# Decays ahead of heads, seven shared banks and warming matmuls in a Mamba, attention and expert layer

## The chip, the cores and the metric

The kernel runs on one core of a Trainium2 chip. The metric is the device time of one execution in microseconds. The core has TensorE (PE; its weight loads are shown as PEld), VectorE (DVE), ScalarE (ACT), GpSimd (POOL) and SyncE (SP, which here only issues transfers). Each engine takes its instructions in the order of its own list and waits on semaphores. TensorE writes to eight PSUM banks of 128 x 512 f32.

## The reference

One decoder layer on x of shape (8, 256, 512), in f32:

```python
x = x + ssm(layernorm(x))                       # Mamba-2: 64 heads of 16, state 128, chunks of 128
x = x + cross_attention(layernorm(x), ctx, ctx) # 32 query heads of 16 on 8 key heads, softmax
x = x + top2_experts(layernorm(x))              # 8 experts, gelu(gate) * up, then down
```

In the first part each chunk of 128 tokens needs, for each head, a 128 x 128 matrix of decays exp(cum_i - cum_j) times C·B, and this matrix times x. In the second, the scores are shifted by each row's maximum before the exponential. In the third, each token goes to two of eight experts.

## The kernel before

The work is cut into pieces such as `("decay", s)` or `("score", i)`. A list `ORDER` holds all pieces of the first two parts. Every engine walks the same list and executes its share of each piece, so the list sets the order on every engine, and a piece that waits holds up all that is behind it on its engine. `mixer_slots` (L95) and `attention_slots` (L234) give each piece a slot number. `whole_order` (L322) sorts them.

**The first part, the mixer** (up to about 600 us) has 32 units: batch b, chunk c and half hf of the heads. A unit has eight steps s, each for four heads, 256 in all. The pieces of a step are: `decay` (L639, a bf16 matmul of 60 rows into a bank of its own, four a round), `bound` (ACT L739, which reads the bank and so frees it), `exp` (ACT L743), `mix_v` or `mix_g` (DVE or POOL, both L748, the product with C·B), and `heads` (L651, for two steps at once, 16 matmuls of 32 columns, which add into a bank that the whole unit shares and that is freed by `yz`, DVE L902). Every fourth slot is a round: the heads of steps i-7 and i-5, then the four decays i to i+3. Around the rounds stand the projections (`x`, `z`: L565), the output projection (`out`: L631), transposes (L570), `x_turn` read by `xdt` (DVE L882), and `ones` (L623), which needs `square` (ACT L733) and `fold` (POOL L950, L951).

**The start of the attention** overlaps the mixer's end. For batch 0 the keys are loaded by `ctx_in` (SP L1483), behind the eight loads of `ecum_in` (SP L1006). `k_hi` (ACT L1122, L1123) waits for this load, `k_lo` (POOL L1430) for k_hi, and `k_turn` (PE L570) for k_lo. The piece `freed` makes ACT and DVE wait for the last projection `z` of the last batch.

**The attention** does 32 items a batch. Side by side run the scores of batch b (`score` L1069, `exponent` ACT L1150, `product` L1078 once in four items) and the row maxima of batch b+1 (`max` L1055, `max_fold` DVE L1250). In the middle of a batch the maxima of half the heads are ready: `nmax` (DVE L1257) and `n_turn` (PE L1061). Beside them the finished batch b-1 goes to the router: `r_stats` (DVE L1287), `r_newton` (14 small POOL instructions), `r_xn` (ACT L1169), `r_turn` (PE L570), `r_logit` (L1095). At the end of the last batch three `keep_warm` pieces do matmuls of ones whose result nobody reads (L1024).

**Banks.** `shared_banks` (L217) walks `ORDER` and gives each piece that writes PSUM the bank that was freed longest ago, with a wait for the piece that reads it last. So any change of order also changes which reader each piece waits for. Mixer and attention pieces share all eight.

**The experts** (from about 940 us) come behind the list, with 39 tiles of tokens.

Of the kernel before, what the change touches and what calls it, by code (L numbers as in the profile page):

```python
# [41 lines left out]
GROUP = 4  # L42
NDECAY = 10
BANKS = 8
# [50 lines left out]
def mixer_slots():  # L95
# [3 lines left out]
    def put(s, *pieces):  # L99
        slots.setdefault(s, []).extend(pieces)  # L100

    for i in range(NS_STEPS + 2 * GROUP):
        if i % GROUP == 0:
            for s in range(i - 2 * GROUP + 1, i - GROUP, 2):
                if s >= 0:
                    put(i, ("heads", s))
            for s in range(i, min(i + GROUP, NS_STEPS)):
                put(i, ("decay", s))
        if 0 <= i - 3 < NS_STEPS:
            put(i, ("mix_v" if (i - 3) % 2 else "mix_g", i - 3))  # L110
        if 0 <= i - 2 < NS_STEPS:
            put(i, ("exp", i - 2))
        for s in range(NS_STEPS):
            if i == s - s % GROUP + s % GROUP // 2:
                put(i, ("bound", s))
# [73 lines left out]
DMA_ONLY = {"ecum_out", "ecum_in", "freed", "mixed", "cum_out", "cum_in", "ctx_in", "n_out", "router_in", "first_expert", "r_store", "out_in", "c_weight_out"}  # L189


def bank_use(stage, *key):
# [12 lines left out]
    if stage == "keep_warm":  # L205
        return (stage, *key), (stage, *key)
# [10 lines left out]
def shared_banks(order, size, use):  # L217

    at = {piece: n for n, piece in enumerate(order)}
    bank, opened_after, last = {}, {}, [None] * size  # L220
    for n, piece in enumerate(order):
        used = use(*piece)
        if used and used[0] not in bank:
            k = min(range(size), key=lambda i: -1 if last[i] is None else at[last[i]])
            if last[k] is not None:
                assert at[last[k]] < n, (piece, last[k])
                opened_after[piece] = last[k]
            bank[used[0]], last[k] = k, used[1]
    return bank, opened_after


def attention_slots():
# [20 lines left out]
    for b in range(NB):  # L253
# [19 lines left out]
        for h in range(2):  # L273
            put(n * (b - 1) + n // 2 * (h + 1) - LEAD + 1, ("nmax", b, h))
            at = n * (b - 1) + n // 2 * (h + 1) - LEAD + 3
            put(at, ("n_turn", b, h))
# [46 lines left out]
def whole_order():  # L323
# [3 lines left out]
    def among(a):  # L327
        for at, end, first, width in ((-54, -40, NS_STEPS - 20, 9), (-40, -33, NS_STEPS - 11, 4.9), (-33, -1, NS_STEPS - 3, 19)):
            if at <= a < end:
# [5 lines left out]
              -25: [("k_hi", 0, 0), ("k_lo", 0, 0)], -24: [("k_hi", 0, 1), ("k_lo", 0, 1)]}  # L335
# [11 lines left out]
def layer_kernel(nc, A, out):  # L347
# [12 lines left out]
    with ExitStack() as top:  # L360
# [81 lines left out]
        work_bank, work_after = shared_banks(ORDER, BANKS, bank_use)  # L442
# [584 lines left out]
        def tensor_attention(e, piece):  # L1027
            stage, *key = piece
            if stage == "keep_warm":
                e.wait_ge(*done("exponent", NB * N_ITEMS - 1))  # L1030
                repeated(e, work(*piece), key[1]).then_inc(piece_done[stage], 1)
# [753 lines left out]
```

## Time and profile before

| | us |
|---|---|
| median of 3 runs | 1380.18 |
| lowest and highest | 1377.15, 1388.65 |
| the profiled execution | 1391.4 |
| its span | 1389.6 |
| its mean granted TensorE clock | 0.948 |

In the rows below, a row of a timeline has its start and duration in us, the engine, the line, what is written and read, and how many instructions it joins. In square brackets stands how long the engine was idle before it and what ended that. A row of windows gives for a stretch its length, then the busy us of each engine with the count of its instructions, then the granted TensorE clock as a share of 2.4 GHz (0.50 is 1.2 GHz), the share of DMA time and GB/s.

### The profile page before, as it was taken

The page shows a single profiled execution, that of the slowest core. Times are in us where ns is not written, and L with a number is a line of the kernel's source. Part 1 is how long each engine was busy: PE and PEld are TensorE (multiplying, and loading weights), DVE is VectorE, ACT ScalarE, POOL GpSimd, SP SyncE. Part 2 cuts the span into 40 slices and gives each one's busy share as a digit, 9 for nine tenths or more (in the row PEclk, how much of TensorE's full clock was granted, in tenths as well). Part 3 has the DMA queues.
Part 4 walks back from the last instruction along what each step waited for, and adds up shares of the span by engine and source line. Part 5 has one row for each costly group of instructions (what it writes and reads, how often), then busy time and mean ns, then how long its engine had stood idle before and what let it go on. Part 6 is the DMA issues. An engine that isn't in the chain of part 4 may idle for free.

```text
span 1389.6 us, 22701 instructions
## 1 busy us (share of the span) xinstructions
PE 1296.1 (93%) x7601; PEld 735.4 (53%) x7601; DVE 823.6 (59%) x1847; ACT 696.2 (50%) x1334; POOL 595.3 (43%) x913
## 2 busy tenths in 40 slices
PE   6799999999999989788999988889999999999996
PEld 4567676766766666443444433234444444444443
DVE  6898989888888877588888789561111111111111
ACT  2768686867676765645777776621111111111110
POOL 1475657566666657672333334641222222222221
PEclk9999999999999999889899898669999999999998
DMA  9100000000000001002111100113344244334222
GB/s 346 31 11 18 11 20 11 19 11 19 9 21 10 21 9 28 1 5 102 36 35 36 36 32 32 33 54 109 67 137 138 56 137 141 89 94 137 47 46 30
DMA packets 49553, 77.31 MB, mean 56 GB/s; under 512 B 19168, under 2 KB 32224, under 8 KB 48416
## 3 DMA queue, kind: packets, MB, share of 16 engines
q1 hardware_dynamic: 39504, 52.43, 10.9%
q0 software_dynamic: 8736, 20.61, 7.7%
q10 hardware_dynamic: 1200, 2.82, 0.5%
q8 instruction: 64, 1.05, 0.3%
q14 instruction: 49, 0.40, 0.1%
HBM read 152.97 MB, written 20.25 MB: 125 GB/s over the span
## 4 chain that ended last, share of the span: by engine, by line
PE 64%; DVE 22%; issue 5%; POOL 4%; ACT 3%; DMA 1%; SPq 1%; POOLq 0%; DVEq 0%; ACTq 0%
PE work_ps L565 10%; PE gate_ps L1563 10%; PE up_ps L1563 10%; PE down_ps L1547 9%; PE work_ps L631 7%; DVE maxes L1250 5%; PE work_ps L570 4%; PE work_ps L1078 3%; DVE conv L752 3%; PE mturn_ps L570 2%; DVE decay L748 2%; PE work_ps L1069 2%; PE work_ps L651 2%; PE work_ps L1055 1%; PE work_ps L1095 1%
## 5 line engine op out<-in xcount | busy, mean ns | idle before, releaser
L565 PE MATMUL work_ps<-xnT,w_in 128*128 128x256 f32 (+1 forms) x1216 | 288.1, 385 | 6.1 <-DVE xdt L882 2.8
L565 PEld LDWEIGHTS work_ps<-xnT,w_in 128*128 128x128 f32 (+1 forms) x1216 | 226.3, 192 | 59.5 <-issue 21.5
L748 POOL TENSOR_TENSOR decay<-decay,cbm 128x512 f32<-128x512 f32 x128 | 184.2, 1442 | 128.5 <-ACT decay L743 127.2
L1651 POOL DMA_INDIRECT out_dram<-y_out,ids x39 | 61.9, 1588 | 335.0 <-DVE row_w L1615 231.7
L1250 DVE TENSOR_REDUCE maxes<-work_ps 128x2 f32<-128x512 f32 x256 | 164.5, 681 | 33.5 <-PE work_ps L1055 32.6
L1630 DVE TENSOR_TENSOR act<-gelu,up_ps 128x512 f32<-128x512 f32 x39 | 26.8, 687 | 253.0 <-PE up_ps L1563 253.0
L1150 ACT ACTIVATE prob<-work_ps 128x512 f32<-128x512 f32 x256 | 142.7, 613 | 52.0 <-PE work_ps L1069 52.0
L743 ACT ACTIVATE decay<-decay 128x512 f32<-128x512 f32 x256 | 161.5, 638 | 12.8 <-DVE xnT L1201 5.3
L739 ACT ACTIVATE decay<-work_ps 128x512 f32<-128x512 f32 x256 | 138.8, 601 | 40.6 <-PE work_ps L639 40.1
L1563 PE MATMUL gate_ps<-w_e,xgT 128*128 x312 | 141.0, 595 | 0.9 <-issue 0.9
L1547 PE MATMUL down_ps<-w_e,actT 128*128 x312 | 140.4, 593 | 0.8 <-ACT actT L1593 0.8
L1563 PE MATMUL up_ps<-w_e,xgT 128*128 x312 | 140.3, 592 | 0.0
L748 DVE TENSOR_TENSOR decay<-decay,cbm 128x512 f32<-128x512 f32 x128 | 121.1, 949 | 29.6 <-ACT decay L743 29.6
L631 PE MATMUL work_ps<-w_out,yz 128*128 128x512 f32 x256 | 128.5, 625 | 2.2 <-DVE yz L902 1.4
L1055 PE MATMUL work_ps<-kT,qT 48*128 48x256 f16 x512 | 94.8, 297 | 8.3 <-ACT qT L1144 2.9
L1622 DVE TENSOR_SCALAR y_out<-down_ps,row_w 128x512 f32<-128x512 f32 x39 | 29.3, 750 | 122.3 <-PE down_ps L1547 122.3
L1563 PEld LDWEIGHTS up_ps<-w_e,xgT 128*128 128x128 f32 x312 | 59.3, 190 | 74.6 <-issue 74.6
L752 DVE SCALAR_TENSOR_TENSOR conv<-work_ps,conv_w,conv 128x255 f32<-128x255 f32 (+2 forms) x240 | 97.4, 468 | 0.7 <-ACT conv L705 0.5
L1069 PE MATMUL work_ps<-qT,kT 49*128 49x512 f16 x256 | 92.2, 430 | 1.7 <-ACT prob L1150 0.6
L1078 PE MATMUL work_ps<-prob,v_aug 128*32 128x512 f32 x512 | 81.8, 716 | 11.0 <-DVE kT L1240 7.8
L1580 ACT ACTIVATE xgT<-mturn_ps 128x512 f32<-128x512 f32 x39 | 23.3, 597 | 137.0 <-PE mturn_ps L570 137.0
L1593 ACT ACTIVATE actT<-mturn_ps 128x512 f32<-128x512 f32 x39 | 23.3, 597 | 128.4 <-PE mturn_ps L570 128.4
(267 smaller groups left out, 1922.6 us busy)
## 6 DMA issues: line engine op xcount, KB each, us to landing
w_e<-c_experts_dram SPq DMA_DIRECT2D x39, 3072.0 KB
normed_tokens<-r_xn SPq DMA_DIRECT2D x17, 256.0 KB, 2.4
out_dram<-x_sb SPq DMA_DIRECT2D x17, 256.0 KB, 2.8
eexp<-ecum_scratch SPq DMA_DIRECT2D x64, 64.0 KB
x_sb<-x_dram SPq DMA_DIRECT2D x1, 3072.0 KB, 15.8
w_in<-c_w_inT_dram ACTq DMA_DIRECT2D x1, 2560.0 KB, 12.5
w_in<-c_w_inT_dram SPq DMA_DIRECT2D x1, 2048.0 KB, 8.1
w_out<-c_w_outT_dram SPq DMA_DIRECT2D x1, 2048.0 KB, 21.5
```

What stands on the lines that cost most here:

```text
L565: m = e.matmul(ps[0:width, at:at + L], w_in[:, k, col:col + width], xnT[b % 2][:, k, :], start=(k == 0), stop=(k == KD - 1))
L631: m = e.matmul(work(stage, tile)[:, :], yz[tile % 2][:, ct, :], w_out[:, ct, :], start=(ct == 0), stop=(ct == NCZ - 1))
L739: e.activation(decay[s % NDECAY][:, :], work("decay", s)[:, :], ACT.Relu, scale=-1.0).then_inc(piece_done[stage], 1)
L743: e.activation(decay[s % NDECAY][:, :], decay[s % NDECAY][:, :], ACT.Exp, scale=-1.0).then_inc(piece_done[stage], 1)
L748: return e.tensor_tensor(four(decay[s % NDECAY]), four(decay[s % NDECAY]), cb, ALU.mult)
L752: return e.scalar_tensor_tensor(o, work("x", b, j)[:, i * L:(i + 1) * L - late], conv_w[:, 2 * j + i, TAPS - 1 - late:TAPS - late], o, ALU ...
L1069: e.matmul(work(*piece)[:, :], kT[b % 3][base:base + PARTS + 1, k, t * P:(t + 1) * P], qT[b % 3][base:base + PARTS + 1, 2 * k:2 * k + 2, : ...
L1078: m = e.matmul(work("pv", b, s % N_ITEMS // 8)[32 * q:32 * q + 32, :], v_aug[b % 2][:, t, 4 * kh + q, :], prob[(s - 3 + q) % 12][:, :], st ...
L1150: e.activation(prob[s % 12][:, :], work("score", s)[:, :], ACT.Exp, scale=DH ** -0.5).then_inc(piece_done[stage], 1)
L1250: e.reduce_max(maxes[b % 2][:, t, first:first + 2], work("max", b, p)[:, :].rearrange("p (h t) -> p h t", h=2), AX.X).then_inc(piece_done[ ...
L1547: m = e.matmul(down_ps[i % 2][:, :], actT[i % 2][:, k, :], w_e[:, bass.ds(place[i], 1), k, 2 * EH:].rearrange("p o n -> p (o n)"), start=( ...
L1563: m = e.matmul(ps[:, :], xgT[i % 2][:, k, :], w_e[:, bass.ds(place[i], 1), k, off:off + EH].rearrange("p o n -> p (o n)"), start=(k == 0), ...
```

## The change

It has three edits.

1. In each round the four decays come before the two pairs of heads.
2. In `whole_order`, `k_hi` and `k_lo` of batch 0 move from slots -25 and -24 to -21 and -20, one round later.
3. `shared_banks` gets a list of banks for each piece: mixer pieces may take all eight, attention pieces the first seven. The eighth is written by matmuls that nobody reads: the three `keep_warm` pieces, which no longer wait for a bank, and six new `warm` pieces of five matmuls, one for each batch from 2 to 7, right before its first `n_turn`.

```diff
@@ mixer_slots
         if i % GROUP == 0:
+            for s in range(i, min(i + GROUP, NS_STEPS)):
+                put(i, ("decay", s))
             for s in range(i - 2 * GROUP + 1, i - GROUP, 2):
                 if s >= 0:
                     put(i, ("heads", s))
-            for s in range(i, min(i + GROUP, NS_STEPS)):
-                put(i, ("decay", s))
@@ shared_banks
-            k = min(range(size), key=lambda i: -1 if last[i] is None else at[last[i]])
+            k = min(allowed(*piece), key=lambda i: -1 if last[i] is None else at[last[i]])
@@ attention_slots
+            if b > 1 and h == 0:
+                put(at, ("warm", b, 5))
             put(at, ("n_turn", b, h))
@@ whole_order
-              -25: [("k_hi", 0, 0), ("k_lo", 0, 0)], -24: [("k_hi", 0, 1), ("k_lo", 0, 1)]}
+              -21: [("k_hi", 0, 0), ("k_lo", 0, 0)], -20: [("k_hi", 0, 1), ("k_lo", 0, 1)]}
@@ layer_kernel
-        work_bank, work_after = shared_banks(ORDER, BANKS, bank_use)
+        work_bank, work_after = shared_banks(ORDER, BANKS, bank_use, lambda stage, *key: range(BANKS if stage in MIXER else BANKS - 1))
@@ tensor_attention
             if stage == "keep_warm":
                 e.wait_ge(*done("exponent", NB * N_ITEMS - 1))
-                repeated(e, work(*piece), key[1]).then_inc(piece_done[stage], 1)
+                repeated(e, work_ps[BANKS - 1], key[1])
+            elif stage == "warm":
+                e.wait_ge(*done("r_init"))
+                repeated(e, work_ps[BANKS - 1], key[1])
```

The changed kernel is three lines longer from L1029 on, so its L1058 is L1055 of before.

TensorE in the round of decays 132 to 135, in the mixer's fifth batch (L651 is heads, L639 the decays, L565 a projection; the brackets name what each waits for). Before:

```order
L623 MATMUL work_ps<-ones,squares 128x1 [waits fold,bound]
L651 MATMUL work_ps<-decay,xdt 32x128 [waits mix_v,mix_g]
L651 MATMUL work_ps<-decay,xdt 32x128 x7
L651 MATMUL work_ps<-decay,xdt 32x128 [waits mix_v,mix_g]
L651 MATMUL work_ps<-decay,xdt 32x128 x7
L639 MATMUL work_ps<-RT,LT 128x512 [waits bound]
L639 MATMUL work_ps<-RT,LT 128x512 [waits taps]
L639 MATMUL work_ps<-RT,LT 128x512 [waits xn_copy]
L639 MATMUL work_ps<-RT,LT 128x512 [waits xdt]
L565 MATMUL work_ps<-xnT,w_in 128x256 [waits carried]
```

After:

```order
L623 MATMUL work_ps<-ones,squares 128x1 [waits fold,bound]
L639 MATMUL work_ps<-RT,LT 128x512 [waits bound]
L639 MATMUL work_ps<-RT,LT 128x512 [waits taps]
L639 MATMUL work_ps<-RT,LT 128x512 [waits xn_copy]
L639 MATMUL work_ps<-RT,LT 128x512 [waits xdt]
L651 MATMUL work_ps<-decay,xdt 32x128 [waits mix_v,mix_g]
L651 MATMUL work_ps<-decay,xdt 32x128 x7
L651 MATMUL work_ps<-decay,xdt 32x128 [waits mix_v,mix_g]
L651 MATMUL work_ps<-decay,xdt 32x128 x7
L565 MATMUL work_ps<-xnT,w_in 128x256 [waits carried]
```

The decays moved ahead of the heads. The last of them opens its bank behind `xdt`, and now the heads stand behind that wait.

ScalarE at the start of the attention (L1122 and L1123 are `k_hi`, L743 and L739 exp and bound of the mixer, L733 the square, L720 a tanh of z). Before:

```order
L720 ACTIVATE zs<-work_ps 128x512
L1122 ACTIVATE xbc<-xbc 128x16x16
L1123 ACTIVATE xbc<-xbc 128x16x16
L743 ACTIVATE decay<-decay 128x512
L739 ACTIVATE decay<-work_ps 128x512 x2
L733 ACTIVATE squares<-yz 128x512
L1122 ACTIVATE xbc<-xbc 128x16x16
L1123 ACTIVATE xbc<-xbc 128x16x16
L743 ACTIVATE decay<-decay 128x512
L739 ACTIVATE decay<-work_ps 128x512 x2
```

After, from the second instruction behind the same L720 on (L1125 is `k_hi` now):

```order
L739 ACTIVATE decay<-work_ps 128x512 x2
L733 ACTIVATE squares<-yz 128x512
L743 ACTIVATE decay<-decay 128x512
L739 ACTIVATE decay<-work_ps 128x512 x2
L743 ACTIVATE decay<-decay 128x512
L726 ACTIVATE state<-work_ps 128x512
L1135 ACTIVATE xn<-x_sb,a_rows 128x512
L1141 ACTIVATE xbc<-xn 128x32x16
L743 ACTIVATE decay<-decay 128x512
L720 ACTIVATE zs<-work_ps 128x512
L1125 ACTIVATE xbc<-xbc 128x16x16
L1126 ACTIVATE xbc<-xbc 128x16x16
```

Two bounds, exponentials, the square and the state's copy now come before the first `k_hi`, which stands behind the second L720.

TensorE at the first `n_turn` of batch 2 (L1061, after L1064), with the product (L1078, L1081), a score (L1069, L1072) and a max (L1055, L1058). Before:

```order
L1055 MATMUL work_ps<-kT,qT 128x256 [waits max_fold]
L1055 MATMUL work_ps<-kT,qT 128x256
L1078 MATMUL work_ps<-prob,v_aug 32x512 [waits exponent,k_copy]
L1078 MATMUL work_ps<-prob,v_aug 32x512 x3
L1061 MATMUL work_ps<-ident,nmax 16x128 [waits nmax,exponent]
L1061 MATMUL work_ps<-ident,nmax 16x128
L1069 MATMUL work_ps<-qT,kT 128x512 [waits max_fold]
L1055 MATMUL work_ps<-kT,qT 128x256 [waits exponent]
L1055 MATMUL work_ps<-kT,qT 128x256
```

After:

```order
L1058 MATMUL work_ps<-kT,qT 128x256 [waits k_copy]
L1058 MATMUL work_ps<-kT,qT 128x256
L1081 MATMUL work_ps<-prob,v_aug 32x512 [waits exponent]
L1081 MATMUL work_ps<-prob,v_aug 32x512 x3
L1024 MATMUL work_ps<-m_ones 128x512 [waits r_init]
L1024 MATMUL work_ps<-m_ones 128x512 x4
L1064 MATMUL work_ps<-ident,nmax 16x128 [waits nmax,max_fold]
L1064 MATMUL work_ps<-ident,nmax 16x128
L1072 MATMUL work_ps<-qT,kT 128x512 [waits exponent]
L1058 MATMUL work_ps<-kT,qT 128x256 [waits max_fold]
L1058 MATMUL work_ps<-kT,qT 128x256
```

The five matmuls of ones (L1024) come between product and `n_turn`. The wait for `k_copy` moved from the product to the max ahead of it.

## Rows read from the trace of the kernel before

**Rows 1.** The page: the span, and the clock granted in 40 slices.
```profile
span 1389.6 us, 22701 instructions
...
PEclk9999999999999999889899898669999999999998
```

**Rows 2.** Windows by stage: mixer, attention, end of the attention.
```profile
50.00:500.00 450.00, 439.30 (x3390) 310.35 (x3389) 384.38 (x725) 329.64 (x651) 284.44 (x399) 1.00 0.06 15
...
640.00:870.00 230.00, 208.45 (x1633) 96.92 (x1629) 195.95 (x497) 169.72 (x323) 75.50 (x180) 0.87 0.14 47
...
884.00:915.00 31.00, 29.65 (x114) 10.57 (x111) 10.54 (x50) 16.70 (x32) 15.63 (x39) 0.50 0.10 35
```

**Rows 3.** Timeline of all engines, 543 to 563 us, where the attention starts.
```profile
547.00 0.59 ACT L720 ACTIVATE zs<-work_ps 128x512 f32<-128x512 f32 x1
...
548.63 1.95 PE L631 MATMUL work_ps<-w_out,yz 128*128 128x512 f32 x4 [0.90 <-DVE yz L902]
...
549.76 3.57 SPq L1483 DMA_DIRECT2D xbc<-ctx_dram  x2
...
552.94 0.42 ACT L1122 ACTIVATE xbc<-xbc 128x256 f16<-128x256 f32 x1 [5.35 <-DMA xbc<-ctx_dram]
...
560.07 0.56 PE L623 MATMUL work_ps<-ones,squares 128*128 128x1 f32 x2 [2.97 <-POOL squares L951]
```

**Rows 4.** Windows with TensorE alone (length, busy us, clock, DMA, GB/s).
```profile
559.87:566.70 6.83, 6.63 (x42) 0.50 0.00 0
```

**Rows 5.** Waits of TensorE from 50 to 500 us: total, times, longest.
```profile
PE work_ps L651 <- DVE decay L748: 4.8, 7, 1.2
```

**Rows 6.** Timeline of TensorE in the round of decays 120 to 123.
```profile
297.61 0.65 PE L651 MATMUL work_ps<-decay,xdt 128*32 128x128 f32 x16 [0.65 <-DVE decay L748]
298.18 0.60 PE L639 MATMUL work_ps<-RT,LT 60*128 60x512 bf16 x4
```

**Rows 7.** Timeline of all engines in the round of decays 132 to 135.
```profile
324.91 0.74 DVE L882 TENSOR_TENSOR xdt<-work_ps,dt_tok 128x256 f32<-128x256 f32 x2
...
326.30 1.99 PE L565 MATMUL work_ps<-xnT,w_in 128*128 128x256 f32 x8 [0.21 <-DVE eexp L889]
```

**Rows 8.** Windows of the attention by half batches, all engines.
```profile
679.00:697.00 18.00, 17.68 (x123) 9.46 (x123) 11.58 (x26) 10.93 (x19) 2.66 (x7) 0.72 0.20 67
697.00:714.00 17.00, 14.87 (x131) 6.22 (x129) 16.76 (x45) 15.29 (x33) 7.69 (x17) 1.00 0.01 1
714.00:731.00 17.00, 15.81 (x121) 8.48 (x120) 11.30 (x26) 10.63 (x19) 2.74 (x8) 0.80 0.21 71
...
782.00:799.00 17.00, 16.97 (x112) 8.80 (x109) 10.17 (x26) 8.83 (x15) 3.25 (x10) 0.61 0.21 72
...
851.00:870.00 19.00, 16.12 (x84) 7.13 (x84) 17.34 (x60) 8.27 (x16) 12.93 (x34) 0.65 0.16 57
```

**Rows 9.** Timeline of TensorE around the first `n_turn` of batch 3.
```profile
712.33 1.06 PE L1078 MATMUL work_ps<-prob,v_aug 128*32 128x512 f32 x8 [1.63 <-DVE kT L1240]
...
716.48 0.72 PE L570 MATMUL work_ps<-ident,r_xn 128*128 128x128 f32 x4 [0.87 <-ACT r_xn L1169]
```

**Rows 10.** Windows with TensorE alone: stretches at half clock behind that place.
```profile
681.40:686.16 4.76, 4.76 (x24) 0.50 0.55 201
716.88:720.30 3.42, 3.42 (x18) 0.50 0.48 177
...
856.25:860.24 3.99, 3.98 (x18) 0.50 0.38 133
```

**Rows 11.** Timeline of all engines, attention, first half of a batch.
```profile
738.67 2.10 ACT L1150 ACTIVATE prob<-work_ps 128x512 f32<-128x512 f32 x4
...
738.74 1.06 PE L1078 MATMUL work_ps<-prob,v_aug 128*32 128x512 f32 x8
...
739.61 2.48 DVE L1250 TENSOR_REDUCE maxes<-work_ps 128x2 f32<-128x512 f32 x4
```

**Rows 12.** Timeline of TensorE: the matmuls of ones at full clock.
```profile
933.17 3.18 PE L1024 MATMUL work_ps<-m_ones 128*128 128x512 bf16 x14
```

More of the change, by code:

```diff
@@ L188, in mixer_slots @@
     return slots
-DMA_ONLY = {"ecum_out", "ecum_in", "freed", "mixed", "cum_out", "cum_in", "ctx_in", "n_out", "router_in", "first_expert", "r_store", "out_in", "c_weight_out"}
+DMA_ONLY = {"ecum_out", "ecum_in", "freed", "mixed", "cum_out", "cum_in", "ctx_in", "n_out", "router_in", "first_expert", "r_store", "out_in", "c_weight_out", "keep_warm", "warm"}
 def bank_use(stage, *key):
@@ L204, in bank_use @@
         return ("score", *key), ("exponent", *key)
-    if stage == "keep_warm":
-        return (stage, *key), (stage, *key)
     if stage == "q_turn":
@@ L214, in bank_use, with shared_banks @@
     return ((stage, *key), (read_by[stage], *key)) if stage in read_by else None
-def shared_banks(order, size, use):
+def shared_banks(order, size, use, allowed):
     at = {piece: n for n, piece in enumerate(order)}
```

## The prediction

> **What bounds the kernel now.** The page comes first: its line of the clock shows full speed in the mixer and in the experts, and less only in slices 19 to 28, about 560 to 950 us [rows 1]. The windows by stage tell who sets the pace. From 50 to 500 us TensorE is busy 439.3 of 450 us at clock 1.00: it is the bound, and only the other 10.7 us can be won there without taking work from it [rows 2]. In the attention nobody is busy all the time: TensorE 208 and VectorE 196 of 230 us, at clock 0.87. The half batches split this up. From 697 to 714 us VectorE works 16.76 of 17 us at full clock, so the maxima set the pace. In 679 to 697 and 714 to 731 us TensorE is busy almost throughout, at 0.72 and 0.80, and VectorE only 11.6 and 11.3 us: there TensorE sets it, and part of its time is the clock's [rows 8]. This pattern comes back each batch. The experts' stage is TensorE at full clock throughout, and the change leaves it alone. Last, the timeline where the attention starts shows one long stall: ScalarE sits 5.35 us for the load of the context [rows 3].
>
> **The k_hi move.** The load is issued at 549.76, behind the loads of `ecum_in`, and lands at 552.9; ScalarE has been free since 547.59. Behind the waiting `k_hi` stand the exponential, two bounds and the square, behind the square the fold on GpSimd, and behind the fold TensorE's `ones`, which waits 2.97 us until 560.07 [rows 3]. Then the clock is at half for 6.83 us, in which TensorE is busy 6.63 [rows 4]; what it did before the fall was to be idle. In the new order two exponentials, four bounds, the square and the state's copy come before `k_hi`. The square then runs at about 549.2, since `yz` is done at 548.6, and the fold is over by 551, before TensorE reaches `ones` at 557.1. `k_hi` comes behind a tanh that needs a projection ending at 557.1, 4 us after the landing, so its wait is gone, not moved. Next in line is `k_turn`, which needs `k_lo`; TensorE reaches it only some ten microseconds behind `ones`. Up to there everything shifts by 2.97 us, plus half of 6.83 us if the clock stays up: **-6.4 us**. If the clock falls anyway it is -3.0. If what follows is late for another reason, 0.
>
> **The decays ahead of the heads.** No instruction is added. Four decays take 0.60 us [rows 6], two pairs of heads about 1.0. It gains where TensorE stands before heads for `mix_v`, for the decays now fill that time, at most 0.60 us of it. The waits of 50 to 500 us have 4.8 us of this kind in 7 places [rows 5], one of them in [rows 6]. The shortest is filled whole with 0.3, one with 0.5 and five with 0.6: 3.8 us. It loses where a decay's bank opens late, as the heads are then behind it. In the round of decays 132 to 135 the last decay needs `xdt`, which ends at 325.65. The heads then end at about 326.7, while the next projection has started at 326.30 [rows 7]: 0.4 lost. This stands alike in batches 4, 5 and 6, and two rounds with `xdt` or `yz` late lose 0.3 and 0.6: 2.1 us in all. Waits behind 500 us are followed by another wait that ends at the same time, so they bring nothing. Net **-1.7 us**. Ends: -5, if earlier decays also bring ScalarE's chain forward so that all 4.8 us go, and +2, if nothing is filled.
>
> **Seven banks.** I took each piece of the attention with the piece that now frees its bank and looked in the trace when that one ended. Most end long before. In the halves set by VectorE some do not. At 738.74 TensorE starts a product [rows 11]. It now waits for the exponential that starts at 738.67 and ends at 739.3, 0.6 later. Product and score then push the next max to an end of 740.96, where VectorE started its fold at 740.21 (it is in the four from 739.61): 0.8 us late. The other late ones of that half, 0.2 to 0.6, hide in this one, for everybody behind has already shifted. Batches 2 to 5 give 0.8 each, batch 6 1.3, batches 1 and 7 0.35 each: **+5.2 us**. Ends: 0, if ScalarE is ahead by as much, and 2.6 a batch, some 16, if they add up. In the halves set by TensorE no opening is late. The Trainium skill (TensorE: Matmul & The Clock Gate, A second HAM failure mode: psum-queue depth-cycling) says that a kernel that cycles through PSUM banks lets TensorE pause between groups so often that its clock swings. This trace does not agree for the halves set by VectorE: with TensorE busy 14.87 of 17 us in many pauses they keep 1.00 [rows 8]. By the row the banks cost 5.2 us, by the rule the price would be that of rival D.
>
> **The warming matmuls.** Fourteen take 3.18 us at full clock [rows 12], so five take 1.1 us, twice that at half clock, and there are six such blocks. Each stands before `n_turn`, and behind it waits the same batch's r_turn. That one could not start before `r_xn`: TensorE stood 0.87 us for it [rows 9], and 0.3 us just before. So 1.2 us of pauses hide 1.1 us of matmuls, where the pauses are as here. I take **+1 us** for all six. With no cover it is +6.6.
>
> **The clock behind them.** In the second halves the clock falls twice: once behind the pauses of 1.63 and 0.87 us [rows 9], once later, among transposes and the router's small matmuls. The block of ones falls into the first place only. From `r_turn` on, the time at half clock there is 4.76, 3.42 and 3.99 us [rows 10], and twice 3.41 in the batches between; one batch has no fall. TensorE is busy throughout, so half of these 19 us comes back: **-9.5 us**. Ends: 0, and all that the clock costs in the second halves: busy time by one minus clock is 5.0, 3.2, 3.2, 6.6 and 5.6 us [rows 8], the second 3.2 being the half from 748 us, which looks like the one from 714: 23.5 us.
>
> **Sum.** -6.4 - 1.7 + 5.2 + 1.0 - 9.5 = -11.4 us. The profiled execution took 1391.4 us, so 1380.0. It is 0.8% above the median of the three. A likely place is the end of the attention, 31 us at clock 0.50 with TensorE busy 29.65 [rows 2]: at full clock 14.8 us of TensorE and 16.7 of ScalarE could be some 14 us shorter, and the three runs differ by 11.5. Nothing in the change touches it directly. I keep the ratio: 1380.18 x 1380.0 / 1391.4 = 1369.
>
> **Rivals.** A is the forecast, at 1361 to 1378 us: 0.45.
>
> B: with the first fall gone TensorE enters the second place earlier and the clock holds there too. The whole 23.5 us come back: -6.4 - 1.7 + 5.2 + 1.0 - 23.5 = -25.4, 1355 us. Against it: the second fall came with TensorE fully busy, so no pause made it. 0.15.
>
> C: the ones do not hold the clock, since the stretch behind them is thin as well. -1.9 us, 1378. For it: one half batch stayed at half clock for two falls in a row, at 0.61 [rows 8]. 0.20.
>
> D, slower: seven banks keep VectorE waiting. With 16 us instead of 5.2 and no clock won it is -6.4 - 1.7 + 16 + 1 = +8.9, 1389 us. If the pauses also pull the clock of the halves at 1.00 to 0.80, 14.87 us of TensorE become 18.6, 1.6 more than the 17 us, six times: +18.5, 1398. It decides from 1.2 us lost a batch on (six times 1.2 against 8.1 - 1). The skill's section named above speaks for it. Against it are the long leads in the rows before. 0.12.
>
> E: the k_hi move brings nothing, for the chain behind it was late anyway: 1375 us. 0.08.
>
> **From this to the numbers.** A measurement of this kernel can tell about 1%, 14 us, from no change. Below 1366.4 us lies all of B, nearly half of A and a little of C: 0.39. Above 1394 lies part of D: 0.05. The rest is 0.56. The range from 1353 to 1389 leaves out the lower part of B and the upper half of D, and spans the bounds of the clock and of the banks.
>
> **What would show it.** ScalarE without a wait for the context, and `ones` without a pause, with the clock at 1.00 from 560 to 567 us. From 50 to 500 us some 2 us less, with few waits of heads. `max_fold` with waits of up to 0.8 us in the first halves. At each block of ones a product, five matmuls, then `n_turn`, and the next stretch at full clock; a half there would mean C. What would make the forecast wrong most is the clock: where it falls hangs on small shifts, here and at the attention's end.

## The result, with the profile after

The changed kernel takes 1391.89 us (median of 20 runs) against 1385.89 us for the kernel before (20 runs, the same hours). The ratio is 1.0044, with a 95% interval from 1.0025 to 1.0064: 6 us slower, where 11 faster were forecast. The profiled execution took 1390.9 us, and that of before 1391.4. The latter was a slow one of its kind (the runs of before span 1377 to 1394, and the slower ones have the lower mean clock), so the two traces differ by 0.5 us, and the other way. Below, the traces say where time goes, and the ratios say how much the whole is worth.

The page of the changed kernel, its span and its clock:

```profile
span 1389.1 us, 22758 instructions
...
PEclk9999999999999999978999998889999999999999
```

The same three windows as in [rows 2]:

```profile
50.00:500.00 450.00, 433.84 (x3325) 304.64 (x3324) 380.58 (x715) 323.50 (x639) 279.50 (x394) 1.00 0.06 15
640.00:870.00 230.00, 205.71 (x1651) 92.79 (x1652) 197.30 (x493) 170.94 (x324) 71.98 (x175) 0.93 0.14 47
884.00:915.00 31.00, 25.65 (x142) 9.21 (x141) 17.30 (x76) 18.55 (x37) 21.61 (x48) 0.84 0.10 35
```

TensorE, the mixer's bound, is busy 433.8 of 450 us there, where it was 439.3: it waits more, though the edit was to fill its waits. The attention's clock went from 0.87 to 0.93, as meant, but the stretch does not get through more work: the scores 0 to 208 take 215.5 us before and 215.9 after.

**The mixer.** From the first `out` (L631) to that of tile 13 the kernel before took 458.95 us (89.60 to 548.55), and the changed one 468.00 (90.40 to 558.40). The groups of TensorE in these stretches: instructions, busy us, mean ns, then the idle time before them and what ended it. Before:

```profile
L631 PE MATMUL work_ps<-w_out,yz 128*128 128x512 f32 x208 | 101.3, 609 | 1.3 <-DVE yz L902 0.5
L651 PE MATMUL work_ps<-decay,xdt 128*32 128x128 f32 x1664 | 57.8, 276 | 7.0 <-DVE decay L748 7.0
L639 PE MATMUL work_ps<-RT,LT 60*128 60x512 bf16 x208 | 33.0, 381 | 0.3 <-DVE yz L902 0.3
```

After:

```profile
L631 PE MATMUL work_ps<-w_out,yz 128*128 128x512 f32 x208 | 101.3, 609 | 4.6 <-DVE yz L902 4.6
L651 PE MATMUL work_ps<-decay,xdt 128*32 128x128 f32 x1664 | 57.7, 276 | 2.1 <-DVE yz L902 0.9 <-DVE conv L752 0.5 <-DVE decay L748 0.5
L639 PE MATMUL work_ps<-RT,LT 60*128 60x512 bf16 x208 | 37.0, 382 | 7.4 <-DVE xdt L882 6.7 <-DVE conv L752 0.6
```

The heads' waits fell by 4.9 us. The decays got 7.1 us of new waits and 4.0 us more busy time, and `out` 3.3 us of new waits. That is +9.5, and it covers the 9.05 us.

The round of decays 36 to 39 shows two of these at once. All engines, before (round from 114.63 on):

```profile
113.20 1.86 POOL L748 TENSOR_TENSOR decay<-decay,cbm 128x512 f32<-128x512 f32 x1
113.25 0.68 DVE L748 TENSOR_TENSOR decay<-decay,cbm 128x512 f32<-128x512 f32 x1
...
114.45 0.74 DVE L882 TENSOR_TENSOR xdt<-work_ps,dt_tok 128x256 f32<-128x256 f32 x2
...
114.63 1.08 PE L651 MATMUL work_ps<-decay,xdt 128*32 128x128 f32 x32
...
115.64 0.60 PE L639 MATMUL work_ps<-RT,LT 60*128 60x512 bf16 x4
```

After (round from 115.50 on):

```profile
114.00 1.27 POOL L748 TENSOR_TENSOR decay<-decay,cbm 128x512 f32<-128x512 f32 x1
114.08 1.74 DVE L748 TENSOR_TENSOR decay<-decay,cbm 128x512 f32<-128x512 f32 x1
...
115.50 0.60 PE L639 MATMUL work_ps<-RT,LT 60*128 60x512 bf16 x3
...
116.34 0.74 DVE L882 TENSOR_TENSOR xdt<-work_ps,dt_tok 128x256 f32<-128x256 f32 x2
...
117.14 0.39 PE L639 MATMUL work_ps<-RT,LT 60*128 60x512 bf16 x1 [1.04 <-DVE xdt L882]
...
117.46 0.43 PE L651 MATMUL work_ps<-decay,xdt 128*32 128x128 f32 x8
```

The round took 1.62 us and takes 3.04. Three decays run at once, the fourth waits 1.04 us for `xdt` and then runs alone. Four decays that are ready together take 0.60 us, and the fourth alone takes 0.39 more, because it has lost its partner: two decays use different rows of TensorE (0 to 59 and 64 to 123) and run side by side. The round of decays 44 to 47 loses 0.7 us in this batch and 0.4 in the next five, mostly by the same loss of a partner. In batches 4 to 6 the first of the two loses 1.0 us, since `xdt` was late there before as well (1.57 us behind the round's start; in batches 1 to 3 it was 0.56, and is 1.58 now).

**The start of the attention** went as forecast. TensorE at `ones`, ScalarE at the first `k_hi` (L1125 now), and the window behind:

```profile
566.78 0.28 PE L623 MATMUL work_ps<-ones,squares 128*128 128x1 f32 x2
...
567.48 0.41 ACT L1125 ACTIVATE xbc<-xbc 128x256 f16<-128x256 f32 x1
...
566.70:574.00 7.30, 7.30 (x57) 4.25 (x56) 2.23 (x7) 3.42 (x8) 3.83 (x8) 1.00 0.00 0
```

No wait of 5.35 and none of 2.97 us, and clock 1.00 [rows 3, 4]. The lag of 9.8 us at tile 13's `out` is 3.4 us at the last `z`.

**The attention by halves.** A window here goes from one score to the sixteenth after it (the last to score 255). First three of the kernel before:

```profile
664.90:678.56 13.66, 11.72 (x109) 5.03 (x105) 13.48 (x33) 12.54 (x26) 7.41 (x16) 1.00 0.01 3
678.56:699.98 21.42, 20.85 (x149) 10.64 (x147) 14.94 (x37) 13.77 (x24) 3.02 (x9) 0.76 0.17 57
...
888.58:910.35 21.77, 21.77 (x84) 8.33 (x81) 4.54 (x25) 12.21 (x22) 11.05 (x34) 0.50 0.13 49
```

After:

```profile
669.67:687.68 18.01, 15.22 (x114) 5.69 (x113) 15.43 (x39) 12.79 (x26) 9.99 (x24) 0.91 0.01 4
687.68:704.17 16.49, 15.68 (x149) 8.44 (x147) 13.08 (x32) 13.66 (x24) 0.42 (x1) 1.00 0.22 73
704.17:720.69 16.52, 13.72 (x114) 5.54 (x113) 15.44 (x39) 12.79 (x26) 8.54 (x21) 1.00 0.00 0
...
894.75:908.09 13.34, 12.23 (x84) 5.23 (x80) 3.65 (x20) 11.48 (x22) 9.28 (x29) 1.00 0.22 80
```

Five of the six second halves behind a block of ones are 16.5 us at clock 1.00, where they took 19.1 to 21.7 (the sixth, from score 208, still has 0.70). From score 32 to 208 they won 21.2 us, and the first halves lost 20.9. The last stretch won 8.4 us.

Behind the attention nothing was changed, and still the traces differ there. From the first matmul into `mturn_ps` to the end the thirteen kernels take 457.8 to 461.3 us, 458.8 before and 461.0 after, and no run tells why. So some 2 us of the difference between the traces lie in a part that no edit touches.

### The profile page after: what moved, and what is told of

It is laid out like the page before. It is cut to its first block, busy times and chain, and to the rows that moved or that the text cites. A ratio compares the mean times of both kernels' runs of the same rounds, so it can differ in the third digit from the quotient of the medians.

```text
span 1389.1 us, 22758 instructions
## 1 busy us (share of the span) xinstructions
PE 1286.6 (93%) x7631; PEld 729.2 (52%) x7631; DVE 827.0 (60%) x1847; ACT 695.6 (50%) x1334; POOL 593.7 (43%) x913
## 4 chain that ended last, share of the span: by engine, by line
PE 63%; DVE 21%; issue 6%; ACT 4%; POOL 3%; DMA 1%; SPq 1%; POOLq 0%; DVEq 0%; ACTq 0%
PE gate_ps L1566 10%; PE up_ps L1566 10%; PE down_ps L1550 9%; PE work_ps L565 9%; PE work_ps L631 6%; PE work_ps L1081 4%; DVE conv L752 3%; DVE decay L748 3%; PE work_ps L570 3%; DVE maxes L1253 3%; PE mturn_ps L570 2%; PE work_ps L1058 2%; PE work_ps L1072 2%; PE work_ps L651 2%; ACT prob L1153 1%
## 5 line engine op out<-in xcount | busy, mean ns | idle before, releaser
L565 PE MATMUL work_ps<-xnT,w_in 128*128 128x256 f32 (+1 forms) x1216 | 286.6, 384 | 6.3 <-DVE xdt L882 3.6
L565 PEld LDWEIGHTS work_ps<-xnT,w_in 128*128 128x128 f32 (+1 forms) x1216 | 225.9, 191 | 55.7 <-issue 21.4
L1253 DVE TENSOR_REDUCE maxes<-work_ps 128x2 f32<-128x512 f32 x256 | 165.9, 682 | 29.2 <-PE work_ps L1058 28.1
L743 ACT ACTIVATE decay<-decay 128x512 f32<-128x512 f32 x256 | 162.3, 641 | 15.0 <-DVE xnT L1204 6.8
L739 ACT ACTIVATE decay<-work_ps 128x512 f32<-128x512 f32 x256 | 139.1, 604 | 19.7 <-PE work_ps L639 19.4
L631 PE MATMUL work_ps<-w_out,yz 128*128 128x512 f32 x256 | 127.0, 619 | 6.1 <-DVE yz L902 4.6
L1058 PE MATMUL work_ps<-kT,qT 48*128 48x256 f16 x512 | 91.7, 290 | 15.1 <-DVE kT L1243 6.8
L1072 PE MATMUL work_ps<-qT,kT 49*128 49x512 f16 x256 | 87.6, 402 | 4.0 <-DVE maxes L1253 3.3
L1566 PEld LDWEIGHTS gate_ps<-w_e,xgT 128*128 128x128 f32 x312 | 56.9, 192 | 58.7 <-issue 58.7
```

Source lines behind the costliest of these rows:

```text
L565: m = e.matmul(ps[0:width, at:at + L], w_in[:, k, col:col + width], xnT[b % 2][:, k, :], start=(k == 0), stop=(k == KD - 1))
L631: m = e.matmul(work(stage, tile)[:, :], yz[tile % 2][:, ct, :], w_out[:, ct, :], start=(ct == 0), stop=(ct == NCZ - 1))
L739: e.activation(decay[s % NDECAY][:, :], work("decay", s)[:, :], ACT.Relu, scale=-1.0).then_inc(piece_done[stage], 1)
L743: e.activation(decay[s % NDECAY][:, :], decay[s % NDECAY][:, :], ACT.Exp, scale=-1.0).then_inc(piece_done[stage], 1)
L1058: m = e.matmul(work(*piece)[:, hh * L:(hh + 1) * L], qT[b % 3][base:base + PARTS, 2 * k + hh, t * P:(t + 1) * P], kT[b % 3][base:base + PA ...
L1072: e.matmul(work(*piece)[:, :], kT[b % 3][base:base + PARTS + 1, k, t * P:(t + 1) * P], qT[b % 3][base:base + PARTS + 1, 2 * k:2 * k + 2, : ...
```

## The experiments

Each ratio is to runs of the kernel before on the same chip. The kernels were measured in three groups, each on one chip and against the same runs of before: khi_only, khi_seven, khi_warm_eight and all_but_swap; swap_only, swap_selected, whole_change_eight and warm_tail_eight; and warm_before_product, warm_two and tail_covered. A difference of two kernels of one group is good to about 0.3%, 4 us, and one across groups is less certain. The last two columns are from the traces: the start of the first score less that of before (637.15), and the time from there to the last score. How early the mixer gets going varies between executions by 1 to 3 us (swap_only's first `out` is 3.0 later), and that is in the former.

| kernel | ratio | 95% | first score | to the last |
|---|---|---|---|---|
| before | 1 | | 0 | 273.2 |
| changed | 1.0044 | 1.0025-1.0064 | +4.1 | 266.8 |
| khi_only | 0.9977 | 0.9950-1.0003 | -4.6 | 273.2 |
| khi_seven | 0.9978 | 0.9961-0.9996 | -3.8 | 267.0 |
| khi_warm_eight | 0.9917 | 0.9887-0.9947 | -4.8 | 259.6 |
| all_but_swap | 1.0010 | 0.9986-1.0034 | -5.0 | 270.7 |
| swap_only | 1.0076 | 1.0050-1.0103 | +9.9 | 266.7 |
| swap_selected | 1.0061 | 1.0029-1.0093 | +3.8 | 264.0 |
| whole_change_eight | 1.0007 | 0.9984-1.0031 | +4.4 | 262.8 |
| warm_tail_eight | 0.9918 | 0.9891-0.9946 | -6.0 | 256.7 |
| warm_before_product | 0.9864 | 0.9831-0.9896 | -3.5 | 253.2 |
| warm_two | 0.9895 | 0.9863-0.9927 | -1.9 | 259.9 |
| tail_covered | 0.9883 | 0.9851-0.9916 | -3.4 | 251.9 |

### The order of decays and heads

**swap_only**: the kernel before with the first edit alone.

```diff
+            for s in range(i, min(i + GROUP, NS_STEPS)):
+                put(i, ("decay", s))
             for s in range(i - 2 * GROUP + 1, i - GROUP, 2):
                 if s >= 0:
                     put(i, ("heads", s))
-            for s in range(i, min(i + GROUP, NS_STEPS)):
-                put(i, ("decay", s))
```

> The kernel before with the decays ahead of the heads in every round, and nothing else. The prediction's term: -1.7 us, at most +2. The traces say: +9 to +10 us at the first piece of out(13), in steps of 1.4 us at each decay behind xdt(b,0,0), 0.4 us at each behind xdt(b,0,1), 0.6 us at each out that now waits for yz, and back by 0.6 us where the heads waited for VectorE or GpSimd. At the end +7 to +10 us, unless the attention, which waits for the context at its start, gives some back.

It is 1.0076, 10.5 us slower, with an interval of 7 to 14. Its trace loses 8.9 us between the same two pieces of `out` (3.0 to 11.9), in the steps named. The term of -1.7 is wrong by its sign. The same edit costs 12.5 us between khi_warm_eight and whole_change_eight below (eight banks, other groups), and 4.7 between all_but_swap and the changed kernel (seven banks): there the first score is 9.1 us later, and 3.9 come back up to the last, for in all_but_swap the clock fell further in the batch from score 160 (halves of 22.89 us at 0.72 and 18.09 at 0.88, against 20.45 at 0.83 and 16.50 at 1.00).

**swap_selected**: is the loss only where a decay waits for `xdt`?

```diff
+            heads = [("heads", s) for s in range(i - 2 * GROUP + 1, i - GROUP, 2) if s >= 0]
+            decays = [("decay", s) for s in range(i, min(i + GROUP, NS_STEPS))]
+            put(i, *(heads + decays if i % 32 in (4, 12, 20) else decays + heads))
```

> The kernel before with the decays ahead of the heads in five rounds of eight, and the heads first in the rounds whose number i modulo 32 is 4, 12 or 20: the two with a decay behind xdt, and the one whose heads feed the yz that out waits for. If these places are the whole loss, the mixer keeps only the gain: -0.6 us in each round 24 of 32, so -3 us at the first piece of out(13) and -2 to -3 at the end. If the order itself slows the chain over ScalarE and VectorE everywhere, the mixer is 2 us or more slower than before. The prediction's step, cover for the heads' waits, gives -3.8 for the same places.

The mixer did not gain 3 us. It lost 1.9 (0.4 to 2.3), and the whole is 1.0061. The groups of TensorE from 89.95 to 550.80 us, in which L629, L649 and L637 are `out`, heads and decays:

```profile
L629 PE MATMUL work_ps<-w_out,yz 128*128 128x512 f32 x208 | 101.3, 610 | 4.6 <-DVE yz L900 4.6
L649 PE MATMUL work_ps<-decay,xdt 128*32 128x128 f32 x1664 | 57.6, 276 | 3.9 <-DVE decay L746 1.9 <-DVE yz L900 0.9 <-DVE conv L750 0.5
L637 PE MATMUL work_ps<-RT,LT 60*128 60x512 bf16 x208 | 34.1, 382 | 0.0
```

The decays' waits are gone, as expected, but `out` waits for `yz` as in the changed kernel. So my expectation was wrong too. The heads' wait stands in the round right before `out(2k, 0)`. The product it waits for and the `yz` that `out` waits for follow each other on VectorE: what gets past the first wait earlier then stands before the second. Two rows each of before and of the changed kernel, batch 1:

```profile
158.52 0.65 PE L651 MATMUL work_ps<-decay,xdt 128*32 128x128 f32 x16 [1.25 <-DVE decay L748]
...
159.84 1.10 PE L631 MATMUL work_ps<-w_out,yz 128*128 128x512 f32 x2
```

```profile
161.89 0.69 DVE L902 TENSOR_TENSOR yz<-yz,zs 128x512 f32<-128x512 f32 x1
...
162.73 1.10 PE L631 MATMUL work_ps<-w_out,yz 128*128 128x512 f32 x2 [0.68 <-DVE yz L902]
```

The rounds whose number modulo 32 is 24 got 0.62 us shorter, and `out` gave 0.54 back. What is left is lost mostly in batches 1 to 3, since there VectorE's product in front of `xdt` takes 1.72 us, nearly as in the changed kernel, and no longer 0.68. So these two orders have nothing to win in the mixer: VectorE is late in these places, and what earlier or less work on it would bring was not tried.

### The k_hi move

**khi_only**: the kernel before with the second edit alone.

> The kernel before with the move of k_hi and k_lo alone. The prediction's steps give -6.4 us: ScalarE without its 5.35 us for the context, TensorE's ones without its 2.97 us, the clock at 1.00 from 560 to 567 us. The trace of the changed kernel says the same for this place: from the piece ones(6,1,1) to the projection z(7,3,1) it won 6.3 us on the kernel before. If the gain is given back in the attention, where VectorE is nearly always busy in the first halves, the time is the same as before (0 to -2 us), with the first score some 6 us earlier and the last score not.

In the trace the last `z` is 6.0 us earlier and the first score 4.6, and that holds to the end of the attention, half by half to 0.1 us. The whole is 0.9977, -3.2 us with an interval of -7 to +0.4. So the gain is not eaten by the attention, though the runs alone can't tell it from none.

### Seven banks and the ones

The next three have the k_hi move and the heads first, so khi_only is their base. **khi_seven** has the banks without the six blocks.

> k_hi moved and seven banks for the attention, no warming matmuls in the batches, decays behind the heads. The prediction's terms: -6.4 + 5.2 = -1.2 us. Rival one, from the trace of the changed kernel: its first halves of a batch are 20.9 us longer in all than before and its second halves 20.3 us shorter. If the banks make the longer first halves, this kernel loses them without the shorter second halves: -6.4 + 20 = +14 us. Rival two: the first halves are longer only because VectorE has left over there what TensorE, now faster, left no time for; then it is -6.4 + 0, as with eight banks.

**khi_warm_eight** has the blocks without the banks (against the changed kernel, in parts):

```diff
-        work_bank, ... lambda stage, *key: range(BANKS if stage in MIXER else BANKS - 1))
+        work_bank, ... lambda stage, *key: range(BANKS))
+    if stage in ("keep_warm", "warm"):
+        return (stage, *key), (stage, *key)
```

> k_hi moved and the six warm pieces of five matmuls, in one of eight banks taken by the common rule, decays behind the heads. The prediction's terms: -6.4 + 1 - 9.5 = -14.9 us. If the seven banks make the longer first halves and the warming the shorter second halves: -6.4 - 20 = -26 us. If VectorE's work, 28.5 us of a batch of 33 in the changed kernel, gives the won time back whatever the banks: -6.4 + 0 to -2, with second halves of 16.5 us at clock 1.00 and first halves of 16.5 us or more.

**all_but_swap** has both.

> The whole change without its first edit: the heads stand ahead of the decays again. The prediction's terms give -9.7 us on the kernel before (+1.7 on the changed one). The two traces say otherwise: in the mixer the changed kernel lost 9.0 us between the first piece of out and that of the last-but-one pair of tiles, and every loss stands at a decay behind xdt or at out behind yz. By that, this kernel is 9 to 10 us faster than the changed one, so some -3 to -4 us on the kernel before. If the loss were made by something else (for instance by transfers or by the attention's keys loaded elsewhere), it would stay, and this kernel would be within 2 us of the changed one, +4 to +6.

khi_seven has the same ratio as its base, 0.9978 to 0.9977. In its trace only the shares of the halves moved, and the clock with them: the first halves of the five batches from score 32 are 15.6 to 19.5 us long (13.7 to 16.6 in khi_only), three of them at 0.83 to 0.92, and the second ones 17.0 to 18.5 (19.2 to 21.7), at 0.88 to 1.00. The five batches take 173.7 us, and 175.4 in khi_only. khi_warm_eight is 0.0060 below its base, -8.3 us (0.9917 is -11.5 on the kernel before, where the prediction's terms give -14.9). With both it is 1.0010, +1.4 us (-2 to +5), where I had expected -3 to -4: the same seven banks that cost nothing alone cost 12.9 us with the ones (1.0010 less 0.9917, in one group). One batch of each with no fall of the clock, first half and second half. With eight banks:

```profile
691.61:706.58 14.97, 13.02 (x115) 5.31 (x111) 14.75 (x38) 12.53 (x26) 8.48 (x21) 1.00 0.01 2
706.58:723.06 16.48, 15.91 (x149) 8.70 (x147) 13.44 (x32) 13.66 (x24) 1.93 (x4) 1.00 0.22 74
```

With seven:

```profile
729.62:746.14 16.52, 13.73 (x116) 5.54 (x114) 15.44 (x39) 12.78 (x26) 8.57 (x22) 1.00 0.01 2
746.14:762.63 16.49, 15.68 (x151) 8.47 (x147) 13.07 (x32) 13.66 (x24) 1.84 (x3) 1.00 0.22 74
```

The first half is 1.55 us longer. The waits in it (total, times, longest), with eight banks and then with seven:

```profile
PE work_ps L1083 <- DVE kT L1245: 1.6, 1, 1.6
...
```

```profile
PE work_ps L1058 <- DVE kT L1243: 1.6, 1, 1.6
PE work_ps L1081 <- ACT prob L1153: 0.5, 1, 0.5
PE work_ps L1058 <- ACT prob L1153: 0.2, 1, 0.2
PE work_ps L570 <- ACT prob L1153: 0.2, 1, 0.2
PE work_ps L1072 <- DVE maxes L1253: 0.2, 1, 0.2
...
DVE maxes L1253 <- PE work_ps L1058: 0.5, 1, 0.5
```

The bank freed by `k_copy` (kT) went to the product (L1083) and now goes to a `max` (L1058), so VectorE, nearly always busy there, waits 0.5 us for maxima. Four more openings are late, and score and max, which also run side by side on different rows, lose 0.7 us of that (TensorE is busy 13.73 us, not 13.02). Besides, the clock fell in four of the six first halves of the changed kernel (18.01 us at 0.91 above) and in four of all_but_swap, against two of whole_change_eight and one of khi_warm_eight, which have eight banks. Three of the four falls begin in or within 1 us of the pause of 1.6 us and cover the block of ones behind it. The fourth is in the half from score 160, 9 us or more ahead of its block. In the four batches before, all four kernels have that same pause, and with eight banks only one in four falls there, so the pause alone does not make the fall. Whether the further waits of seven banks do was not tested.

**whole_change_eight** is the changed kernel with eight banks.

> The whole change, but the attention keeps eight banks and the ones take a bank by the common rule. By the prediction it is 5.2 us faster than the changed kernel. By the two kernels just measured with and without the eighth bank (heads first in both), the seven banks cost 16.7 us from score 32 to score 208, of which 8.3 came back at the end where the clock happened to stay up: 8 to 16 us faster than the changed kernel. On khi_warm_eight it should be 9 to 10 us later at the first score (the swap), so some -3 us on the kernel before.

1.0007 against 1.0044 (other chips): the banks cost some 5 us in the changed kernel, give or take 4, and not the 8 to 16 expected. In the traces it is 10.4 us ahead from score 32 to 208, and 7.5 us behind from there to the first matmul into `mturn_ps`, since its last half is at clock 0.50. All three kernels with seven banks had that half at 0.98 to 1.00, in one trace each. Of the eight with eight banks that leave the end as it was, five had it at 0.50 and three (swap_only, swap_selected, warm_before_product) at 0.71 to 0.82, so the banks are not the only way to it. Which small shift decides was not found.

### What the ones hold, and what limits a batch then

**warm_before_product**: the block goes ahead of the product that waits for kT.

```diff
-                put(at, ("warm", b, 5))
+                put(at - 0.5, ("warm", b, 5))
```

> khi_warm_eight with its six blocks of five matmuls moved ahead of the score and the product in front of them, so that they stand ahead of the 1.63 us in which TensorE waits for k_copy. If TensorE's own time limits a batch, the 1.1 us of each block are now hidden and a batch takes 30.35 us, not 31.45: 6.6 us less for six, and up to 1.5 us more where the clock fell at the block of the batch from score 96 on. If VectorE limits it (14.76 of 14.97 us busy in these halves), nothing is won by hiding the block: 0 to -1.5 us. If the pauses behind the block (0.4 to 0.9 us ahead of r_turn) are what made the clock fall, the second halves go back to 18 to 21 us and the kernel is 10 to 20 us slower.

**warm_two**: `("warm", b, 2)`.

> khi_warm_eight with two matmuls of ones in each of the six blocks, not five. If what holds the clock is that TensorE has no long pause there, two matmuls (0.45 us) fill half of the 0.87 us ahead of r_turn and the clock holds in some batches only: 3 to 10 us slower than khi_warm_eight. If any block does, it is 4 us faster, 0.65 us a batch. If two are as good as none, the time is that of khi_only, 8 to 14 us slower.

A batch of the one and of the other, and one of swap_only, which has no ones, all at clock 1.00:

```profile
692.75:706.74 13.99, 13.11 (x115) 5.47 (x110) 13.79 (x36) 12.54 (x26) 7.70 (x17) 1.00 0.01 2
706.74:724.10 17.36, 16.30 (x151) 8.70 (x148) 14.36 (x36) 13.77 (x24) 2.74 (x8) 1.00 0.21 69
```

```profile
694.52:708.89 14.37, 12.43 (x113) 4.99 (x109) 14.16 (x38) 12.54 (x26) 7.97 (x18) 1.00 0.01 2
708.89:725.87 16.98, 15.92 (x150) 8.66 (x149) 13.97 (x34) 13.77 (x24) 2.47 (x6) 1.00 0.21 72
```

```profile
779.62:793.29 13.67, 11.71 (x109) 5.05 (x106) 13.50 (x33) 12.53 (x26) 7.37 (x15) 1.00 0.01 2
793.29:810.94 17.65, 16.29 (x149) 8.64 (x148) 14.63 (x38) 13.77 (x24) 3.04 (x9) 1.00 0.21 70
```

The first two batches take 31.35 us each, and with five matmuls behind the product it is 31.45. TensorE's work differs by up to 1.1 us between the three, and VectorE's is 28.1 to 28.2 in all. In swap_only, without any ones, the one batch whose clock stayed at 1.00 takes 31.32 us (from score 128). So at full clock the batch no longer depends on TensorE's work, and the ones cost nothing. That VectorE's chain sets the 31.4 us is what the rows suggest, and no run with less work on VectorE was made. Two matmuls kept four of the five second halves at 1.00, where I had expected some only and 3 to 10 us more time than in khi_warm_eight (0.9895 against 0.9917, other groups); five behind the product all five (four in whole_change_eight), and five ahead of it four (the other at 0.91). Without ones and with eight banks none of the five stayed up in the kernel before and in khi_only, one in swap_only and two in swap_selected. So the ones hold the clock far more often than it holds by itself, and neither always nor only they do. warm_before_product, at 0.9864, has the lowest ratio of the study (1366.7 against 1386.1 us), with an interval that reaches into those of warm_two and tail_covered: the k_hi move, the ones in a shared bank ahead of that product, the heads first, eight banks. Its lead over khi_warm_eight (0.9917, another group) is 7.3 us where at most 1.5 were expected, and its batches do not explain it. Its last half does for the traces, 14.8 us and not 21.8.

**warm_tail_eight** adds a block where TensorE stood 2.07 us before the clock's last long fall.

```diff
+    put(233.5, ("warm", 8, 9))
```

> khi_warm_eight with one more piece of nine matmuls of ones ahead of score 234, where TensorE stood 2.07 us for ScalarE and the clock then was at half from 865 to 896 us with TensorE busy throughout. If the pause makes the fall, the half from score 240 to 255 takes 13.3 to 14 us, not 21.8, and the kernel is 8 to 10 us faster than khi_warm_eight. If the clock falls there whatever TensorE does in the pause, it is 0 to 1 us slower.

Its ratio is that of khi_warm_eight (0.9918 and 0.9917, other groups), where 8 to 10 us less were expected. The clock held there, and fell 10 us later behind the next pause of 1.82 us. The halves from score 224 and 240:

```profile
854.49:867.32 12.83, 10.93 (x70) 3.27 (x69) 11.27 (x42) 9.24 (x19) 10.58 (x21) 1.00 0.02 2
867.32:887.87 20.55, 18.02 (x85) 7.85 (x81) 5.80 (x33) 11.98 (x22) 12.59 (x36) 0.67 0.14 52
```

**tail_covered** covers the other three pauses too.

```diff
+    put(n * (NB - 1) + 16 + 7 + 0.5, ("warm", 9, 8))
+    put(n * NB + 4.5, ("keep_warm", 0, 8)) 
+    put(f, ("attend_v", NB - 1))
-    put(f, ("attend_v", NB - 1), ("keep_warm", 0, 8))
-    ... ("c_rank", 3), ("keep_warm", 1, 5), ("c_count", 3)
+    ... ("c_rank", 3), ("keep_warm", 1, 12), ("c_count", 3)
```

> warm_tail_eight with the other pauses of the attention's end covered too: eight matmuls of ones ahead of r_turn(6,0) (TensorE stood 1.82 us there and the clock then was at half from 874.7 to 888), the first keep_warm ahead of the last pv_turn (1.41 us) instead of behind it, and twelve instead of five ahead of c_count(3) (1.92 us, after which eleven matmuls took 4.85 us at half clock). If the pauses make the falls, the stretch from score 240 to the experts, 40.6 us in warm_tail_eight, takes 32 to 35 us, and the kernel is 5 to 8 us faster than that one. If others are late next (ScalarE's and GpSimd's chains there), the clock is up but the stretch no shorter: 0 to -2 us.

```profile
870.01:885.65 15.64, 14.80 (x93) 5.98 (x89) 5.60 (x33) 11.60 (x22) 12.13 (x35) 0.95 0.18 68
885.65:910.05 24.40, 18.18 (x77) 9.43 (x74) 15.66 (x76) 5.60 (x10) 7.86 (x10) 0.68 0.19 66
```

The half from score 240 is 5 us shorter, and the stretch behind it, up to the first matmul into `mturn_ps`, 4.3 us longer (24.40 against 20.07): TensorE now stands 3.7 us for ScalarE there, and the clock is at half again behind that. In the sum it is 40.04 and 40.62 us, where 32 to 35 were expected if the pauses were all. The ratios, 0.9883 and 0.9918 in different groups, are within each other's error.

## Why the prediction was wrong

- **The decays ahead of the heads**: the step that failed. It forecast -1.7 us, at worst +2, and swap_only measured +10.5. Three parts of it. First, the gain of 3.8 us was right in size (the heads' waits fell by 4.9), but it is passed on: `out` waits 3.3 us more for `yz` on the same late engine. I had checked this only behind 500 us. Second, the loss in the round of decays 132 to 135 was put at 0.4. I let the heads follow `xdt` at once and left out the decay itself, 0.39 us alone; the round took 1.0 us more (3.02 for 2.00). Third, I looked for late `xdt` only in the old trace and found none in batches 1 to 3. There VectorE's product now collides with GpSimd's, and `xdt` is 1.0 us later relative to the round. With the rounds of `xdt(b, 0, 1)`, 0.4 to 0.7 each, the six batches lose 10.0 us, and all decays 11.1 (7.1 of waits and 4.0 of busy time), where I had 2.1.
- **The k_hi move**: right by the traces, in mechanism and size. 9.8 to 3.4 us of lag is the -6.4 forecast, to the tenth; ones without a wait and clock 1.00. Of the 6.0 us in khi_only 1.4 are gone by the first score. The runs of khi_only give -3.2, and their interval holds both the forecast and nothing, so against rival E there is the trace alone.
- **Seven banks**: +5.2, with ends 0 and 16. Measured: 0 with the clock low, +5 in the changed kernel, +12.9 with the heads first. In a clean batch 1.55 us, not 0.8, because the late openings do add up to more than the longest of them. The mechanism of D was there, at a price near its end, but without its condition that the clock is not won. D's further step, that the clock of the halves at 1.00 is pulled down, came true in four of six first halves of the changed kernel (0.83 to 0.91) and of all_but_swap (0.72 to 0.91). The forecast had no term for it. The Trainium skill (TensorE: Matmul & The Clock Gate, A second HAM failure mode: psum-queue depth-cycling) would have the clock swing through the short pauses of such cycling. The rows agree in part: with seven banks a first half full of them is at 1.00 (16.52 us), yet four of six first halves had a fall, against one or two of six with eight banks and the same blocks.
- **The ones**: +1 forecast, and close to 0 by the batches of 31.32, 31.35 and 31.45 us with none, two and five of them, at full clock.
- **The clock**: -9.5 forecast, with rival B at -23.5. B's mechanism is what happened: with the first fall gone the second went too, five second halves are at 1.00 throughout. But B's price was wrong, as was the way of pricing: the cold time comes back only as long as TensorE sets the pace. The five batches from score 32 take 175.4 us before and 161.7 in khi_warm_eight, 2.7 us less each and not 4.7; three of them are the clean 31.45. For ones and clock together the runs of khi_warm_eight show -8.3 us and its trace -13.6 (khi_only's traced execution took 1386.7 us, its median is 1380.0, so the trace shows too much); my two terms gave -8.5. That is luck: the second falls went as in B, and the floor of 31.4 us a batch took back a part of what that was worth.
- **The sum** of the measured parts, 10.5 - 3.2 - 8.3 + 5.1 = +4.1, agrees with the +6.0 of the whole within its error. By it the first term has 12 us of the 17 between -11.4 and +6. Another way round it has less, for the parts do not simply add. all_but_swap, without this term, was forecast at -9.7 and measured at +1.4: of these 11 us 7.7 are the banks' (12.9 and not 5.2) and 3.2 the k_hi move's. So the slowdown that is clear of noise came with the decays, and the forecast gain would have been missed without them too, by the size of the banks' term above all.

The rivals had a case against every edit but this one: the slower kernel, at 0.12, was to come from the banks alone. A term of -1.7 with ends of -5 and +2 had looked too small to need one. The time came out near D's 1389 us for another reason than D's.

One reading of the rows was off: the line of the clock is below 9 in slices 17 to 27 and in the last, not in 19 to 28. No term hangs on it.

## What to carry over

Before moving work ahead of a wait, look at what the waiting engine does next: if one and the same engine is late for both, the wait only moves. An instruction that can be held up by a bank should not stand ahead of one that can't, and its own time alone, without its partner on the other rows, is part of the price. And the worth of a faster clock is the time until the next engine limits the loop, found by changing the work of the fast one and watching whether the loop's time moves.

## What was not expected of the hardware

- A small shift decides who pays when GpSimd and VectorE multiply at once. In batch 1 both begin within 0.1 us: before, VectorE took 0.68 and GpSimd 1.86 us, and after, VectorE 1.74 and GpSimd 1.27. So each needs 0.68 and 1.27 when it wins. The loser takes about its own time plus the rest of the other's, so nothing is shared. The Trainium skill (SBUF — State Buffer, SBUF: two separate sides) calls the port pair of these two engines an exclusive lock that is held for a whole instruction by whoever starts first. The durations agree. Who starts first can't be read here: GpSimd's start is the earlier one in both traces, by 0.05 and 0.08 us.
- Of two decays on different rows of TensorE, the second costs next to nothing when both are ready, and 0.39 us when it comes later. The Trainium skill (TensorEngine Tiling (Array Packing), Key Properties) says that such tiles run independently; the price of a partner that waits is this trace's: 4.0 us more of busy time, with 14 such rounds of 52 where there were four.
- Two matmuls of ones (0.45 us, by 0.22 from one start to the next) kept the clock at 1.00 over a half batch of 17 us in four of five. With eight banks and no ones it stayed there in none to two of five.
